# Fetching each tile of edges once, with the blocks of nodes in natural order, in a four-layer graph network

## The reference, cut to what matters

```python
h = relu(layernorm(x)); x = x + L0(h)   # 8-head attention by scores, then batch norm, feed-forward, batch norm
h = relu(layernorm(x)); x = x + L1(h)   # filter layer: msg = (h W)[src] * ((rbf W_r2m + b) * C(edge_weight))
h = relu(layernorm(x)); x = x + L2(h)   # one-head attention, logit = (h Wn)[src].attn + (edge_attr We).attn
h = relu(layernorm(x)); x = x + L3(h)   # GCN: msg = (h W)[src] * dinv[src] * dinv[dst]
# in every layer: agg = segment_sum(msg, dst)
```

## Time and profile before

| | us |
|---|---|
| median of 3 runs | 5746.98 (5736.75 to 5750.54) |
| span of the profiled execution | 4836.7 |
| index work and node stage, to the first gather | 0 to 192.6 |
| edge stage 1, then layer 0's tail (attention out, feed-forward, table 1) | 192.6 to 1629.6 |
| edge stage 2 (filter), by its first gather | from 1629.6 |
| edge stage 3 (one-head attention), by its first gather | from 2700.4 |
| edge stage 4 (GCN), by its first gather | from 3780.8 |

### The profile page before, as it was taken

How to read it: one execution, slowest core, us unless ns; L and a number is a source line. 1 busy time by engine, 2 the same in 40 slices (tenths; PEclk the granted TensorE clock), 3 DMA queues, 4 the chain that set the end, 5 groups by cost and what they waited for, 6 DMA issues and landing times. The chain is left out here.

```text
span 4836.7 us, 67940 instructions
## 1 busy us (share of the span) xinstructions
PE 3551.4 (73%) x13730; PEld 2548.5 (53%) x13730; DVE 3365.7 (70%) x9609; ACT 2021.2 (42%) x5849; POOL 3211.3 (66%) x3433
## 2 busy tenths in 40 slices
PE   8888777787798677767666578888888555555555
PEld 5566555565654455555555355555555444444444
DVE  7799999999833677777777477777777444444444
ACT  2466666666543433333333466666666000000000
POOL 1477777777200377777777577777777577777776
PEclk9866777867899878888888677777777677777777
DMA  3254454445300444444443244444443233333333
GB/s 118 89 139 136 138 139 138 139 138 139 90 16 3 119 122 127 125 125 125 126 125 108 80 111 113 114 114 114 114 114 109 80 111 112 112 112 112 111 112 100
DMA packets 346051, 540.75 MB, mean 112 GB/s; under 512 B 75816, under 2 KB 237899, under 8 KB 345675
## 3 DMA queue, kind: packets, MB, share of 16 engines
q0 software_dynamic: 146432, 386.15, 28.6%
q1 hardware_dynamic: 191755, 142.86, 10.3%
q10 hardware_dynamic: 7488, 7.72, 0.5%
HBM read 506.37 MB, written 30.07 MB: 111 GB/s over the span
## 5 line engine op out<-in xcount | busy, mean ns | idle before, releaser
L747 POOL DMA_INDIRECT e_rows<-table,src_idx x2496 | 2360.7, 946 | 1079.0 <-issue 538.8
L811 DVE TENSOR_TENSOR acc<-acc,banks 128x273 f32 (+3 forms) x3328 | 1298.9, 390 | 819.4 <-PE banks L799 646.0
L799 PE MATMUL banks<-e_rows,e_hot 128*128 128x128 f32 (+1 forms) x3328 | 990.0, 440 | 705.9 <-DMA e_rows<-table,src_idx 442.6
L799 PEld LDWEIGHTS banks<-e_rows,e_hot 128*128 128x128 f32 x3328 | 754.6, 256 | 935.1 <-DMA e_rows<-table,src_idx 484.6
L747 POOL DMA_INDIRECT edge_rows<-table,src_idx x832 | 800.5, 962 | 256.1 <-issue 188.5
L799 PE MATMUL banks<-edge_rows,e_hot 128*128 128x273 f32 x1664 | 728.3, 569 | 13.2 <-DVE edge_rows L1259 12.3
L799 PE MATMUL banks<-e_rows,e_weighted_hot 128*128 128x257 f32 x1664 | 645.5, 520 | 16.5 <-ACT e_weighted_hot L962 16.0
L926 ACT ACTIVATE e_apart<-const,dst_loc 128x128 bf16<-128x128 f32 x1664 | 505.9, 388 | 15.4 <-PEq L527 9.1
L799 PEld LDWEIGHTS banks<-edge_rows,e_hot 128*128 128x128 f32 x1664 | 385.9, 264 | 104.5 <-DVE acc L811 19.2
L799 PEld LDWEIGHTS banks<-e_rows,e_weighted_hot 128*128 128x128 f32 x1664 | 366.3, 249 | 108.3 <-issue 29.0
L962 ACT ACTIVATE e_weighted_hot<-e_hot,e_weight 128x128 f32<-128x128 f32 x832 | 254.3, 388 | 9.8 <-issue 1.1
(11 more groups left out here) (314 smaller groups left out, 4961.4 us busy)
## 6 DMA issues: line engine op xcount, KB each, us to landing
e_edge_in<-in_edge_attr SPq DMA_DIRECT2D x832, 80.0 KB
e_rows<-table,src_idx POOLq DMA_INDIRECT x2496
e_node_rows<-node_line SPq DMA_DIRECT2D x104, 256.0 KB, 3.4
edge_rows<-table,src_idx POOLq DMA_INDIRECT x832
table<-n_row SPq DMA_DIRECT2D x49, 132.0 KB, 1.7
table<-fn_row ACTq DMA_DIRECT2D x49, 129.0 KB
X<-in_x SPq DMA_DIRECT2D x1, 6272.0 KB
values<-table SPq DMA_DIRECT2D x49, 128.0 KB, 2.0
```

The source lines that it names most:

```text
L747: nc.gpsimd.indirect_dma_start(out=rows[:, u, q, 0:width], out_offset=None, in_=table, in_offset=bass.IndirectOffsetOnAxis(ap=at, axis=0)) ...
L799: nc.tensor.matmul(banks[:, 2 + q % turn, 0:width], onehot, rows, start=True, stop=True).then_inc(summed_tile, 1)
L811: nc.vector.tensor_tensor(at, at, banks[:, 2 + q % turn, 0:width], ALU.add).then_inc(added, 1)
```

## The change

Three things change. First, the blocks go round in natural order, from a starting block that the index work looks for, so that every tile belongs to one or two neighbouring steps and a bound known beforehand tells how far the tiles can be behind the steps (`newest`, `needed`). Second, in the two plain stages each tile is gathered once, 784 in 98 groups of eight instead of 832, into a ring of 64 tiles, and PE reads the slot of each of its eight steps from a register. In the filter stage the loads of edge attributes, the scaling, the filters, the filtered rows and the logits go by the 98 groups too; in 6 of the 104 batches (19, 35, 52, 69, 86 and 103) `fresh` is None and no new group is needed. Third, since `edge_q` is then in the order of groups, the third edge stage reads it with one register for each tile. To make room, `hot` and `logit_part` of the filter stage, `hidden` of the feed-forward and two small tensors of layer 0's tail move into unused parts of `acc`. The cutoffs are turned by 7 transposes and go through DRAM instead of being split and picked.

```diff
+WORK = TILES + NB - 1          # 830
+FETCHED = TILES + 1
+FETCHES = -(-FETCHED // G)     # 98
+FETCH_W = FETCHES * G          # 784
+HELD = 64
+FETCH_RING = HELD // G
+SPARE = HELD - 2 * G
+def newest(s):
+    at = min(s, WORK - 1)
+    ranks = -(-NB * (at + 1) // WORK) - 1
+    return at if ranks == 0 else at - ranks + 1
+def needed(j):
+    return newest(j * G + G - 1) // G
+def fresh(j):
+    if j >= BATCHES or j > 0 and needed(j) == needed(j - 1):
+        return None
+    return needed(j)
+def last_use(g):
+    return min(g + NB - 1, WORK - 1)
...
+        def fetch_tiles(pool, table, width, rows, fetched, summed_tile, spare_read=()):
+            for g in range(FETCH_W):
+                if g == SPARE:
+                    for read, count in spare_read:
+                        pool.wait_ge(read, count)
+                if g >= HELD:
+                    pool.wait_ge(summed_tile, summed(0, last_use(g - HELD)))
+                nc.gpsimd.indirect_dma_start(out=rows[:, g % HELD, 0:width], out_offset=None, in_=table,
+                                             in_offset=bass.IndirectOffsetOnAxis(ap=src_fetch[:, g:g + 1], axis=0)).then_inc(fetched[g // G % FETCH_RING], 16)
...
+        def load_slots(j):
+            return nc.values_load_multi_w_load_instructions(
+                slot_line[:, bass.ds(j * G, G)], engines=[PE_ENGINE], min_val=0, max_val=HELD - 1,
+                skip_runtime_bounds_check_because="cut to the ring's size when they were made")[1]
```

In the third edge stage (`value` and the register reads of the DVE, `ROW_REGS` goes from 12 to G + 2 + G):

```diff
-                                v.tensor_tensor(sums[:, 0, :].unsqueeze(2), rows[:, u, :, D + 1:D + 2], edge_q[:, bass.ds(n * G, G)].unsqueeze(2), ALU.add).then_inc(logit_ready, 1)
+                                for q in range(G):
+                                    last = v.tensor_tensor(sums[:, 0, q:q + 1], rows[:, u, q, D + 1:D + 2], edge_q[:, bass.ds(fetch_at[q], 1)], ALU.add)
+                                last.then_inc(logit_ready, 1)
...
+                if self.with_fetch:
+                    self.fetch_at = fetch_places((n + 2) % BATCHES)   # 8 registers, a second read
...
-                        ahead = RowAhead(G if many else ROW_REGS)
+                        ahead = RowAhead(G if many else G + 2, not many)
```

In the plain stages (PE):

```diff
-                            sum_tile(pe, j, q, hot[:, u % 2, q, :], rows[:, u, q, :], summed_tile, added, width, sum_banks)
+                            row = rows[:, bass.ds(slots[q], 1), :].squeeze(1)
+                            sum_tile(pe, j, q, hot[:, u % 2, q, :], row, summed_tile, added, width, sum_banks)
...
+                            one, two, slots = fresh(j + 1), fresh(j + 2), load_slots(j)
...
-                            if filtered and inside(j + 1):
-                                make_filters(j + 1, (u + 1) % 2)
+                            if filtered and one is not None:
+                                make_filters(one, one % 2)
```

At the ends of the filter stage's POOL program and of the node stage's SP program, and in the index work on POOL:

```diff
+                            nc.gpsimd.memset(unsummed[:, 0:3 * G, :], 0.0)
...
+                        sp.wait_ge(cut_tiles_ready, 1)
+                        keep_twice(cutoff_line, cut_tiles)
+                        sp.wait_ge(tiles_out, 64)
...
-                    nc.gpsimd.tensor_scalar(step_tile, tile_k[TILE_LINE:TILE_LINE + 1, 0:BATCHES * G], float(TILES - 1), None, ALU.min)
+                    (4 operations of 784 elements on one partition after "begin", then 8 of up to 832 after "block")
...
-                        if many:
-                            pick_cutoff()
```

More of the change, by code:

```diff
@@ L345, in _ @@
                     dve.wait_ge(idx_dve, now)
-                    now = step(v.scalar_tensor_tensor(size_key[:, :], length[:, :], 64.0, block_of[:, 0:NB], ALU.mult, ALU.add))
+                    now = step(v.tensor_reduce(begin[:, 0:1], size_key[:, :], AX_X, ALU.max))
+                    own = ident[0:NB, 0:NB]
+                    for c, line in enumerate((prefix[0:NB, :], first_tile[0:NB, 0:NB], length[0:NB, :])):
+                        v.scalar_tensor_tensor(spread[:, c, :], own, 1.0, line, ALU.mult, ALU.mult, accum_out=own_size[:, c:c + 1])
@@ L347, in _ @@
                     dve.wait_ge(idx_dve, now)
-                    own = ident[0:NB, 0:NB]
-                    for c, line in enumerate((size_key[0:NB, :], first_tile[0:NB, 0:NB], length[0:NB, :])):
-                        last = v.scalar_tensor_tensor(spread[:, c, :], own, 1.0, line, ALU.mult, ALU.mult, accum_out=own_size[:, c:c + 1])
-                    now = step(last)
+                    v.scalar_tensor_tensor(spread_all[:, 0, :], size_key[:, :], begin[:, 0:1], prefix[:, :], ALU.is_equal, ALU.mult, accum_out=begin[:, 1:2])
@@ L498, in _ @@
                     spread_keys(P - 1, 6, ends_spread)
+                    pe.wait_ge(firsts_kept, 1)
+                    for g in range(GROUPS):
+                        last = nc.tensor.transpose(banks[:, 4 + g // 4, g % 4 * P:(g % 4 + 1) * P], end_f[:, 1, g, :], ident)
+                    last.then_inc(src_turned, 1)
                     pe.wait_ge(restart_ready, 1)
@@ L606, in _ @@
                             last.then_inc(product, 1)
+                            if b == 44:
+                                pe.wait_ge(cut_steps, 6)
+                                for g in range(GROUPS):
+                                    last = nc.tensor.transpose(banks[:, 6 + g // 4, g % 4 * P:(g % 4 + 1) * P], cut[:, g, :], ident)
+                                last.then_inc(cut_turned, 1)
                     @blk.vector
@@ L1501, in batch @@
                                 node.act_keep(act, k)
[L1502 to L1503 removed]
+                            if filtered and two is not None:
+                                keep_scaledT(two, two % 2)
                         if filtered:
@@ L1682, in batch @@
                                 node.dve_row(dve, last)
-                            if filtered and inside(j + 1):
-                                filter_rows(j + 1, un, 0)
+                            if filtered and one is not None:
+                                filter_rows(one, 0)
                             add(3)
@@ L2019, in add_and_filter, with _ @@
                 with nc.Block() as blk:
+                    @blk.gpsimd
+                    def _(pool):
+                        nc.gpsimd.memset(acc[:, NB - HIDDEN_BLOCKS:NB, :], 0.0)
                     @blk.sync
```

310 lines of the change are left out of this document (185 added, 125 removed).

## The result

The changed kernel takes 5834.66 us (median of 4 runs, 5803.05 to 5856.22) where the kernel before takes 5741.86 us (4 runs, 5733.06 to 5750.54): a ratio of 1.0175, 95% interval 1.0136 to 1.0214. It is slower by 93 us; the prediction said 5713 us, 34 us faster than 5747.

A forecast was written before the change was run, and what follows sets the result against it. POOL's indirect gathers, 1.25 us each, were taken as the bound, with stage 3 close to DVE-bound. -55 - 54 + 65 + 10 = -34 us, from 5746.98 to 5713 us; range 5640 to 5800.

The forecast's parts named there:

- 910.3 us: Time of the timed runs around the profiled span; left unchanged and added to the predicted span.
- stage 3's pace over 1.42 us: Sign that the forecast is wrong: stage 3's time per gather above 1.42 us, where 1.3 to 1.4 was expected.
- Stages 2 and 4, -55 and -54: 48 gathers fewer each at 1.249 us save 60.0 us of POOL time, less 5 and 6 us given back.
- the window does not close: Stages 2 and 4: the new ring lets gathers start 16 steps after the needed sum, against 32, without delaying POOL.
- Rival (c): Stage 2 doesn't follow: PE's slot reads or the narrower ring lose its 55 us; 5768 us, chance 0.05.
- the 69 us of the bound: Stage 2: at worst PE's register read and eight slot addresses cost 0.66 us a batch, 69 us for 104 batches.
- Stage 3, +65: Eight adds and a second register read add 1.3 us a batch, 0.68 hidden by slack, over 104 batches: +65 us.
- rival (b): Stage 3's DVE adds and second register read take more than is saved: slower, 5812 us, chance 0.18.
- If a read costs the same whatever it carries: Stage 3: upper bound for reading six more registers, 0.66 us a batch instead of 0.33.
- neither end: Stage 3's bounds for reading six more registers: 0.2 us if the two reads overlap, to 0.66 us.
- The start, +10: Before the edge stages: index work +4 us, node stage's stores +5 and PE's seven transposes +1, together +10 us.
- keeps its gathers and its batches: 0: Stage 1: gathers and batches stay as they are, so its time changes by 0.

The follow-up runs named there:

- e1_before: The kernel before, unchanged, profiled again on the first chip: 5606.43 us, with a span of 5604.6 us.
- e10_fewer: The kernel before with six batches' gathers left out in each of stages 2 and 4 (784 instead of 832), nothing else changed: 0.9862 of before.
- e4_both: Changed kernel with stage 3's adds back to one, no second register read, and fixed ring places for slot registers in stages 2 and 4: 0.9966 of before.
- e2: Changed kernel with stage 3's eight adds put back to one add of eight, without the second register read: 0.9987 of before.
- e3_fixed_slots: Changed kernel with TensorE reading stages 2 and 4 from fixed ring places instead of slot registers: 1.0120 of before.

## Why the prediction was wrong, point by point

- **The profile and the timed runs.** This is the step that failed: "The timed runs have 910.3 us around that span; I leave it as it is, since no row tells what it is." The 910 us did not lie around the span. Between e1_before and that profile 768 us lie inside the stages, 154 to 224 us in each, and 2 us outside, in an execution that POOL's 1.25 us does not bound. That the span fell short of the runs by 16% stood in the table of times, and the text even said that it might spoil all. It should have put a chance on "the timed runs are not bound as this profile is" and then given the POOL saving only in part. One of its own signs of being wrong, stage 3's pace over 1.42 us, was met: 1333.6 us from the first to the last gather there, 1.60 each. (In reading it also gave all of POOL's idle time to the issue; the row gives it 538.8 of 1079.0 us.)
- **Stages 2 and 4, -55 and -54.** The saving was sized at 1.25 us a gather. Alone it measured 77 us for 96 (e10_fewer), 0.8 us each. In the change it came to +7 and -24 us (e4_both against e1_before), slot registers left out. The ring was argued to be wide enough, "the window does not close". It does: the 65th gather waits 54 us in stage 2 and 32 in stage 4. That the ring also lets 64 gathers go first was not thought of, and pacing gave some 53 us back. Rival (c), "stage 2 doesn't follow", had this outcome, and it named POOL's waiting in the narrower ring. But pacing makes POOL wait sooner and gains, so it isn't that wait that costs. Slot registers cost 12 us (e4 against e2), well under the 69 us of the bound.
- **Stage 3, +65.** The mechanism of rival (b) was right and my size for the forecast was not. The eight adds are 0.79 us (predicted 7 x 0.13 + 0.06 beyond the one that was there, the right order). Of stage 3's terms the reads were the mis-sized one: 0.33 us was taken for six more registers, and they came to about 2 us, from 0.85 for the one read to 1.69 + 1.24, the means of (1.07, 2.30) and (0.61, 1.86). "If a read costs the same whatever it carries" was nearer, but neither end had that a read costs by where its row starts. Of the added 2.7 us a batch, e3_fixed_slots against e4_both shows 84 us, 0.8 us a batch, in stage 3 (1364.1 - 1279.9); what hides the rest wasn't tested; the late signals that the DVE waits for anyway could. Rival (b)'s 5812 us lies nearest to the result, by a stage 3 cost sized too high and a saving that was not there.
- **What a register read costs.** The Trainium skill (Runtime: NRT & Kernel Launch, "Instruction fetch mechanics") has about 200 ns a register. No read here goes by the register: 12 take 0.85 us, 10 take 1.07 and 8 take 0.59, and two to three times that off the multiple of 16.
- **The start, +10.** The first gather comes at 198.67 instead of 192.59: +6 us, near enough. Stage 1, "keeps its gathers and its batches: 0", was held to that by its profile: 1632.9 in e3_fixed_slots against 1635.0 in e1_before, although both engines' reads in it had doubled on average. Of the 299 us by which it looked longer, some 200 are what e1_before has too, and the rest is within what stage 1 differs by from chip to chip.
- **The sum for the change**, from the ratios: reads off the multiple of 16, 1.25%; adds and second read, 1.0%; slot registers, 0.2%; the ring of 64 without pacing, 0.95% (53 us of 5604); the fewer gathers, -1.4%. That is 2.0%, where 1.75% to 2.0% was measured. It fits better than it has to: the parts come from three chips and are not independent, and each has some 0.2% of uncertainty.

Not settled: how the change stands on a chip like the fifth, where the POOL-bound sum could still hold. It was not run there.

## What to carry to other kernels

Set the profiled span against the timed runs before summing anything: a gap of 16% says that the profile shows another bound than the one you will be timed on, and that is a rival with a large chance, not a constant. When a table that registers are read from gets wider rows, keep each row's start at a multiple of 16 bytes. A ring that is made larger for reuse also lets its producer run further ahead; tie the run-ahead to what is needed, separately from the ring's size. When chips differ, price a part only against a run on the same chip: here the comparison across chips made 85 us of 53.

## What the runs showed of the hardware

- A register read of 8 words takes 0.59 us (stage 1) from a row at a multiple of 16 bytes and 1.85 (DVE) to 1.94 us (TensorE) from one 8 bytes off; 12 words take 0.85 and 2.73 us, and 10 words 1.06 and 2.3 us (stage 2), so ten take longer than twelve when both are on the multiple.
- On four chips, while POOL issues gathers every 1.25 us without a wait, TensorE and the DVE finish a sum only about every 5 us. TensorE's signals are then recorded 3.0 to 4.4 us after the modelled end of the matmul (e1_before and the changed kernel), and even a signal from the DVE to itself can come 1.6 us late (3700.92 + 0.21 to 3702.74 in the changed kernel). When POOL pauses, they do a sum in about 1 us. On a fifth chip none of this is seen, and the kernel takes 14 to 16% less.
